# A 16-head causal attention with a gated feed-forward layer: another fixed order on all five engines, and P*V of two units moved behind the next pair's first scores

## What is computed

```python
# attention, x: (4, 1024, 128), 16 heads of 64
q = (x @ Wq).reshape(B, N, H, Dh).transpose(0, 2, 1, 3)
kv = x @ Wkv                      # k and v alike
s = jnp.einsum('bhid,bhjd->bhij', q * scale, k)
gm = jnp.max(s, axis=-1, keepdims=True)          # over the whole row
p = jnp.where(causal_mask, 0.0, jnp.exp(s - gm))
out = jnp.einsum('bhij,bhjd->bhid', p, v) / (jnp.sum(p, axis=-1, keepdims=True) + EPS)
x = layernorm(x + out.reshape(B, N, H * Dh) @ Wo + bo)
# feed-forward: x_prev is x one token earlier
xr = mu_r * x + (1 - mu_r) * x_prev;  xk = mu_k * x + (1 - mu_k) * x_prev
r = sigmoid(xr @ W_r);  k_act = square(relu(xk @ W_k))
x = layernorm(x + r * (k_act @ W_v))
```

## Time and profile before

| | |
|---|---|
| median of 3 runs | 1035.9 us (1035.74 to 1036.77) |
| the profiled execution | 1036.35 us, its span 1034.6 us |
| busy share of the span | PE 93%, weight loads 67%, DVE 88%, ACT 68%, POOL 57% |
| granted TensorE clock | 0.993 of full speed on the mean |
| a usual step of the main loop | 29.7 us |
| main loop ends | at about 970 us; the rest is the tail |

### The profile page before, as it was taken

One profiled execution on the slowest core, in us unless ns is written; L12 is line 12 of the kernel. 1 busy time (PEld: TensorE's weight loads), 2 busy tenths in 40 slices (PEclk: granted clock), 3 DMA queues, 4 the chain that ended last, 5 costly groups with the idle time before them and its releaser, 6 DMA issues. The chain is left out here.

```text
span 1034.6 us, 24773 instructions
## 1 busy us (share of the span) xinstructions
PE 966.7 (93%) x8947; PEld 689.2 (67%) x8947; DVE 910.2 (88%) x1546; ACT 704.5 (68%) x1456; POOL 586.1 (57%) x918
## 2 busy tenths in 40 slices
PE   7799999999999999999999999999999999999895
PEld 5566666676766666667666666767666766666463
DVE  5989888998898899889889988898899889889957
ACT  4667667666676666667667666766666667667667
POOL 5345655565656556555655565665556556653363
PEclk9999999999999999999999999999999999999898
DMA  6255665556556545555564555556555555665432
GB/s 171 57 140 130 137 153 129 121 121 145 133 130 148 132 118 129 137 138 133 140 153 115 117 135 138 134 134 153 135 122 121 135 140 134 140 150 131 100 81 82
DMA packets 74218, 134.24 MB, mean 130 GB/s; under 512 B 26864, under 2 KB 36848, under 8 KB 74096
## 3 DMA queue, kind: packets, MB, share of 16 engines
q1 hardware_dynamic: 73520, 132.26, 54.6%
q10 hardware_dynamic: 576, 0.39, 0.2%
HBM read 21.17 MB, written 2.36 MB: 23 GB/s over the span
## 5 line engine op out<-in xcount | busy, mean ns | idle before, releaser
L879 DVE TENSOR_SCALAR_CACHE_REDUCE tile<-ps 128x1024 f32<-128x1024 f32 x512 | 599.5, 1217 | 90.7 <-PE ps L1137 90.5
L682 ACT ACTIVATE tile<-tile,neg_max 128x640 f32<-128x640 f32 (+7 forms) x512 | 393.3, 770 | 128.7 <-POOL tile L487 128.6
L1137 PE MATMUL ps<-ks,qs 64*128 64x512 f32 x3072 | 398.8, 397 | 9.3 <-DVE tile L879 3.8
L1137 PEld LDWEIGHTS ps<-ks,qs 64*128 64x128 f32 x3072 | 294.4, 184 | 73.1 <-issue 28.9
L487 POOL TENSOR_SCALAR_AFFINE_SELECT tile<-tile 128x128 f32<-128x128 f32 x512 | 151.1, 295 | 302.9 <-DVE tile L879 302.8
L1250 PE MATMUL ps<-pt,vs 128*64 128x256 f32 (+1 forms) x2560 | 264.6, 361 | 0.8 <-DVE tile L879 0.5
L888 DVE STREAM_TRANSPOSE stage<-tile 128x640 f32<-128x640 f32 (+3 forms) x256 | 250.5, 1015 | 0.0
L1250 PEld LDWEIGHTS ps<-pt,vs 128*64 128x64 f32 x2560 | 173.7, 137 | 101.8 <-DVE tile L879 14.2
L1176 PE MATMUL ps<-xs,ws 64*128 64x512 f32 x744 | 119.5, 425 | 22.4 <-DVE tile L879 16.9
L495 POOL TENSOR_TENSOR ot<-ot,rb 128x512 f32<-128x512 f32 x64 | 101.6, 1588 | 55.5 <-issue 54.5
L689 ACT ACTIVATE x1t<-ps 128x1024 f32<-128x1024 f32 x31 | 31.9, 1028 | 125.4 <-PE ps L1176 125.4
(11 more groups left out here) (91 smaller groups left out, 587.5 us busy)
## 6 DMA issues: line engine op xcount, KB each, us to landing
pt<-stage SPq DMA_DIRECT2D x512, 120.0 KB, 3.2
pt<-stage SPq DMA_DIRECT2D x512, 88.0 KB, 2.1
rb<-recips SPq DMA_DIRECT2D x64, 256.0 KB, 4.1
y<-in_L_attn_x SPq DMA_DIRECT2D x3, 512.0 KB, 8.7
out<-y SPq DMA_DIRECT2D x3, 512.0 KB, 3.2
pt<-in_L_attn_Wkv SPq DMA_DIRECT2D x2, 384.0 KB, 6.8
pt<-in_L_attn_x SPq DMA_DIRECT2D x2, 256.0 KB, 4.4
wos<-in_L_attn_Wo SPq DMA_DIRECT2D x1, 512.0 KB, 7.2
```

What stands on the lines that cost most here:

```text
L682: act.activation(cols, cols, ACT.Exp, bias=neg_max[:, at:at + 1], scale=-1.0, accum_out=sums[:, p % 2, a, t:t + 1]).then_inc(s_exp, 1)
L879: dve.tensor_scalar(tile[:, at, :], place_for(("scores", p, t, a))[:, :], -SCALE, None, ALU.mult, ALU.min, accum_out=neg_max[:, at:at + 1] ...
L1137: ins = mm(place_for(("scores", p, t, a))[:, c * HALF:(c + 1) * HALF], qs[rows, p % 2, qh, t * P:(t + 1) * P], ks[rows, p % 2, kh, c * HAL ...
```

## The change

It has three parts. The set of instructions of the loop stays the same; all of them are moved.

**PE's list and the places.** K's projection of the next pair comes first in step k and alternates half by half with v's; q's two halves stand around scores 2; the output projection's two halves stand around group 2, late in the step. PV0 of pair k moves to step k+1, behind its scores 0. PV1 of the pair before moves up, behind scores 4, and scores 5 is cut in its halves by group 1. The table `FOLLOWS` is new throughout; the parts of it that matter here: k follows PV0, q follows scores (1, 0), scores (3, 0) follows q, group 1 follows PV1, scores (7, 0) follows the output projection, scores (7, 1) group 2.

**The other lists.** DVE, ACT and POOL get the order that goes with it. DVE's transposes of tiles 6 and 7 of a pair now stand behind the next step's first readings. `norm(k-1, 1)` stands between the masks of tile 7 on POOL.

**SP's list.** The moves of units 2 and 3 stand together, and the two DMAs of the reciprocals come behind the last move of unit 3.

**The tail.** PV0 of pair 31 comes behind the loop and takes the first place in `LATE`; on ACT `take_out(30)` and `take_values(31, 0)` stand ahead of the first square root.

```diff
 FOLLOWS = {
-    ("scores", 3, 0,): (("out",), 2),
+    ("scores", 3, 0,): (("q",), -1),
-    ("scores", 7, 0,): (("pv", 0,), 0),
-    ("scores", 7, 1,): (("scores", 6, 1,), 0),
-    ("q",): (("scores", 0, 0,), 1),
-    ("k",): (("scores", 2, 1,), 1),
+    ("scores", 7, 0,): (("out",), 2),
+    ("scores", 7, 1,): (("group", 2,), 0),
+    ("q",): (("scores", 1, 0,), 1),
+    ("k",): (("pv", 0,), 2),
-    ("group", 1,): (("scores", 3, 1,), 0),
+    ("group", 1,): (("pv", 1,), 1),
...
-LATE = [("out", LAST, 0), ("pv", LAST, 1), ("pv", LAST, 2), ("out", LAST, 1), ("sum", 3, 0), ("sum", 3, 1)]
+LATE = [("pv", LAST, 0), ("out", LAST, 0), ("pv", LAST, 1), ("pv", LAST, 2), ("out", LAST, 1), ("sum", 3, 0), ("sum", 3, 1)]
...
+                move(k, 2, 0)
+                move(k, 2, 1)
+                move(k, 2, 2)
+                move(k, 2, 3)
+                move(k, 3, 0)
+                move(k, 3, 1)
+                move(k, 3, 2)
+            move(LAST, 3, 3)
             column_recips(LAST)
-            move(LAST, 3, 0)
             spread_recips(LAST)
-            move(LAST, 3, 1)
-            move(LAST, 3, 2)
-            move(LAST, 3, 3)
...
             mask(LAST, 7, 1)
             add_out(LAST - 2, 1)
+            norm(LAST - 1, 0)
             norm(LAST - 1, 1)
...
+            take_out(LAST - 1)
+            take_values(LAST, 0)
             deviations(0, 0)
             take_last_sums(0)
...
-            turn_sums()
             project_out(LAST - 1, 0)
             project_out(LAST - 1, 1)
+            values(LAST, 0, (0, 1))
+            turn_sums()
             turn_normed(0, 0)
```

More of the change, by code:

```diff
@@ L44 @@
 LAST = ALL_PAIRS - 1
+SUMS_IN = "kq"
 def x_half(p):
@@ L514, in _ @@
             for k in range(ALL_PAIRS):
+                if k >= 1:
+                    mask(k - 1, 0, 0)
+                if k >= 1:
+                    mask(k - 1, 0, 1)
+                if k >= 1:
+                    mask(k - 1, 1, 0)
+                if k >= 1:
+                    mask(k - 1, 1, 1)
+                if k >= 3:
+                    norm(k - 3, 0)
+                if k >= 1:
+                    mask(k - 1, 2, 0)
+                if k > 0:
+                    split(k, 0)
+                if k >= 1:
+                    mask(k - 1, 2, 1)
+                if k >= 1:
+                    mask(k - 1, 3, 0)
+                if k >= 1:
+                    mask(k - 1, 3, 1)
+                if k > 0:
+                    split(k, 1)
+                if k >= 1:
+                    mask(k - 1, 4, 0)
+                if k > 0:
+                    split(k, 2)
+                if k >= 1:
+                    mask(k - 1, 4, 1)
+                if k >= 1:
+                    mask(k - 1, 5, 0)
+                if k >= 1:
+                    mask(k - 1, 5, 1)
                 if k > 0:
                     split(k, 3)
+                if k >= 3:
+                    add_out(k - 3, 0)
+                if k >= 1:
+                    mask(k - 1, 6, 0)
                 if k >= 1:
@@ L520, in _ @@
                     mask(k - 1, 7, 0)
+                if k >= 2:
+                    norm(k - 2, 1)
                 if k >= 1:
                     mask(k - 1, 7, 1)
[L523 to L540, removed]
                 if k >= 3:
                     add_out(k - 3, 1)
[L543 to L549, removed]
+            mask(LAST, 0, 0)
+            mask(LAST, 0, 1)
+            mask(LAST, 1, 0)
+            mask(LAST, 1, 1)
+            norm(LAST - 2, 0)
+            mask(LAST, 2, 0)
+            mask(LAST, 2, 1)
+            mask(LAST, 3, 0)
+            mask(LAST, 3, 1)
+            mask(LAST, 4, 0)
+            mask(LAST, 4, 1)
+            mask(LAST, 5, 0)
+            mask(LAST, 5, 1)
+            add_out(LAST - 2, 0)
+            mask(LAST, 6, 0)
             mask(LAST, 6, 1)
@@ new lines, in _ @@
+            evacuate(LAST, 2, 0)
+            evacuate(LAST, 2, 1)
+            evacuate(LAST, 3, 0)
+            evacuate(LAST, 3, 1)
+            evacuate(LAST, 4, 0)
+            recips_of(LAST - 1)
+            evacuate(LAST, 4, 1)
+            weights_of_mix()
+            evacuate(LAST, 5, 0)
+            evacuate(LAST, 5, 1)
+            turn_tile(LAST, 4, 0)
+            turn_tile(LAST, 4, 1)
+            evacuate(LAST, 6, 0)
+            evacuate(LAST, 6, 1)
+            first_moments(0)
@@ L1346, in _ @@
                 if k < LAST:
+                    project_qk(k + 1, "k", 0)
+                else:
+                    turn_half(0, 0)
+                project_values(k, 0)
+                if k < LAST:
+                    project_qk(k + 1, "k", 1)
+                else:
+                    turn_half(0, 1)
+                project_values(k, 1)
+                if k < LAST:
                     project_qk(k + 1, "q", 0)
                 else:
-                    turn_half(0, 0)
+                    turn_half(1, 0)
+                scores(k, 2, 0)
+                scores(k, 2, 1)
                 if k < LAST:
```

272 lines of the change are left out of this document (137 added, 135 removed).

## The result

The changed kernel takes **1051.95 us** (median of 4 runs, 1051.63 to 1054.22) against 1035.82 us for the kernel before in the same session (4 runs, 1035.32 to 1036.77). The ratio is 1.0159, 95% interval 1.0146 to 1.0172: slower by 1.6%. The forecast was 1045.5 us, in a range of 1034 to 1056. The profiled execution took 1052.2 us with a span of 1050.3 us, 15.7 more than the 1034.6 before, and all that follows accounts for these 15.7.

A forecast was written before the change was run, and what follows sets the result against it. PE, hardly ever stopping, was taken to bound the loop. The loop's -10.4 us and the tail's +20.2 us gave +9.8 us on the profiled 1036.35 us, 1045.5 us after allowing 0.45 us for the median; range 1034 to 1056 us.

The forecast's parts named there:

- the clock's rival: Tail: half clock after PE's two stops slows PV0 by 2.3 us and later work by some 3; 1051 us, chance 0.15.
- Gone, -1.4 us a step: Main loop: alternating k and v, and moving other calls between halves, removes PE waits of 1.4 us a step.
- New, behind q, 0.7 us: Each step, ahead of scores 3: PE waits 0.7 us for ACT's copy of q, covered only by group 0.
- The first rival: Main loop: steps are shorter than forecast, 28.5 us if q's copy is ready; 1024 to 1034 us, chance 0.15.
- New, ahead of scores 6, 0.25 us: Each step: scores 6 wait 0.25 us for the place of scores (5, 1), which DVE must read first.
- A usual step, 29.25 us: Main loop: 28.3 us of PE work plus waits of 0.7 and 0.25 us, 0.46 us less than before.
- Six steps with turned tokens, 1.55 us each: Group 1 waits for ACT's copies and DVE's subtraction: 0.6 us work and 0.95 us wait extra in each.
- Step 0 is bound by DVE in both, 0: First step of the loop: DVE bounds it before and after the change, so its time changes by 0 us.
- The tail (a) to (c), 22.8 us: Later pair 30 output projection, table load 13.9 us later, reciprocals behind 16 moves: norm (31, 0) starts 22.8 us later.
- the second rival: Tail: reciprocals are no bound if PE and POOL find work during SP's moves; 1036.6 us, no change, chance 0.13.
- (d), 2.6 us given back: Tail, after norm (31, 0): work gathered during the wait is then ready and gives back 2.6 us.
- The steps gain nothing: Main loop: PV2 waits for SP's moves, or scores 6 and 7 for readings; 29.75 us steps, 1060 us, chance 0.15.

The follow-up runs named there:

- kernel 6: Changed kernel with the second half of q's projection ahead of scores 2, next to the first: 1074.23 us.
- kernel 7: Changed kernel with k's two halves side by side and v's two behind them, alternation undone: 1070.59 us.
- kernel 8: Changed kernel with 20 and 28 matmuls of no use in step 0, where PV1 and PV2 stand in later steps: 1049.78 us.
- kernel 5: Changed kernel with DVE subtracting turned tokens ahead of its reading of scores (4, 1), not behind it: 1044.03 us.
- kernel 11: Kernel 10 with 16 more matmuls of no use in each of steps 0 and 1, where the output projection stands in later steps: 1025.17 us.
- kernel 1: Changed kernel with the last pair's reciprocals sent behind unit 2's moves and fetched behind unit 3's first 4 moves, as before: 1042.50 us.
- kernel 2: Changed kernel with ACT's first two square roots ahead of the copies of pair 30's output and PV0 of pair 31: 1040.01 us.
- kernel 3: Changed kernel with the edits of kernel 1 and kernel 2 together: 1036.91 us, ratio 1.0002 to before.
- kernel 4: Kernel before with only the last pair's reciprocals going out and back behind all 16 moves of unit 3: 1045.33 us.
- kernel 9: Changed kernel with the edits of kernel 1, kernel 2 and kernel 5: 1027.52 us, ratio 0.9923 to before.
- kernel 10: Kernel 9 with the matmuls of no use of kernel 8 in step 0: 1026.56 us, ratio 0.9904 to before.

## Why the prediction came out as it did

The sign and the mechanism held: the loop gained, the tail lost more, by the chain that was foretold, and the time lay in the range. It lay above the 1040 to 1050 us that the forecast alone reaches. That the clock's rival says 1051 us is luck: it counted stops of the tail, and much of what was missed lies in the first steps. 1051.95 - 1045.5 = 6.5 us were missed, by these steps:

- **Gone, -1.4 us a step: right in kind, too small.** I priced a pair side by side against half of a pair of scores, 1.53 us. The measure of a projection without the wait is its own, 1.38 us, so both pairs together cost 0.9 us and not 0.6. Kernels 6 and 7 give 0.33 to 0.34 for one pair moved back: a pair takes 1.71 to 1.72 us there and took 1.83 in the kernel before, and no run shows where that last 0.1 us comes from.
- **New, behind q, 0.7 us: right** (0.75, in every step and in kernels 7 and 8). That the place of scores (2, 0) sets a floor only 0.3 us below it I didn't see; kernel 6 showed it. The first rival (steps under 28.9 us) falls with it, by a little: 29.03.
- **New, ahead of scores 6, 0.25 us: the wrong place.** The wait is 0.4 us, one call earlier, ahead of the output projection. It inherits from scores (4, 1), and scores 6 then come late enough for theirs.
- **A usual step, 29.25 us: 29.03.** This gave 30 x 0.22 = 6.6 us that I hadn't counted on, and it hid as much of the misses below: that the loop's sum came near is in part luck, errors that cancel.
- **Six steps with turned tokens, 1.55 us each: mis-sized, 2.35.** The wait is 1.64 us, where I had 0.95, and scores 6 and 7 wait for readings on top: +0.8 each, 4.8 us over the six. Kernel 5 took back 7.2.
- **Step 0 is bound by DVE in both, 0: this failed.** PE has less to do in it than before, since PV0 of pair 0 left it, and stands in front of scores 5; its clock falls. +1.85 us, and a low clock in step 1 costs 2.8 more (34.2 us, against 31.4 for a token step); step 10 lost 1.0, at a granted clock of 0.89 on the mean of the 15 us from 330. The step that failed is the one that put PE's clock at nothing in the loop: I looked for it only in the tail. Kernels 8 and 11, with the stops of step 0 filled, run it at the full clock and begin step 1 at 41.13 and 41.31 us.
- **The tail (a) to (c), 22.8 us: right in each link, 20.9.** The output projection at 37.35 (38.5 predicted), the table load at 45.8 (46.9), the end of the last transpose at 52.9 (54.4), 16.8 us from there (17.1). My 17.1 was a little below its own terms: 8.2 + 8 us and at least 1 for the landing make 17.2 to 18.7. Kernels 1 to 4 show both causes, one by one and together: the second rival falls with kernels 1 and 4, in which SP's order alone took back 9.5 us and cost 9.2.
- **(d), 2.6 us given back: failed.** The work was ready, and the last output projection started 1.57 us after norm instead of 2.78. But it took 2.08 us instead of 1.02, and PV1 3.80 instead of 2.60, at a clock of 0.51: +2.3 us. The clock's rival was right on this stop. Behind the first one PV0 took 2.38 us, and that was luck: the same two stops (8.4 and 1.1 to 1.2 us) stand in the profiles of all eleven kernels with the new order, and PV0 took 2.38 us in four of them (after, 6, 7, 9) and 3.77 to 4.53 in seven.
- **The steps gain nothing: wrong.** PV2 never waited for SP's moves in a usual step.

In sum, step 0 +1.85, the loop +2.8 (-6.6 + 4.8 + 3.8, and 0.8 because the 24 usual steps take 29.06 us on the mean and not 29.03), the tail +1.2: 5.9 us in the span. The rest is how the two profiled executions lie to their medians, and a slip: 1036.35 + 9.8 - 0.45 is 1045.7, not 1045.5. What I hadn't joined up is that a long stop which the new order opens in the loop can be paid for twice, once as a wait and once as slow matmuls behind it.

## What to carry to other kernels

When a loop is reordered, write its last pass separately and keep there the order that its consumers need: here two DMAs behind twelve moves in one pass of 32 cost 9 us, more than the 7.5 that the loop's new order won. Price a wait by the instruction's own time without it, not by that of a similar one. And count what follows a stop on PE at the half clock as well as at the full one, in the first steps too, where a reordering takes the work away that kept PE running. A single profile can fall on either side: compare the same stretch in several kernels before giving its difference to an edit.

## What the hardware showed that I had not expected

**A loop that looks busy can drop to the half clock.** After: PE stops for 2.35 us in step 0, the granted clock is 1.00 up to 32.0 us and 0.50 from 32.5 to 38.5, and the 24 matmuls in that stretch take 4.64 us instead of 3.0. The stops of 0.66 and 0.76 us lie inside the low stretch and came too late to cause it. In kernel 8 the clock fell near 64 us, behind a stop of 1.56 us in step 1 and ahead of one of 1.41, and the same 24 matmuls took 5.25 us.

**The same stops don't always do it.** In the kernel before, two stops of 1.88 and 1.94 us stand close together ahead of step 1, and the clock stays at 1.00. PV0 of pair 31 is the case above: 2.38 us after and 4.53 in kernel 5, behind equal stops and with the same program in the tail; the clock was back at 1.00 when it began in the one and came back only at its end in the other. Kernels 9 and 10 have equal stops in step 1 (0.4, 0.2 and 1.6 us). In 9 the 24 matmuls behind them take 3.06 us, in 10 they take 4.61:

```profile
67.18 3.06 PE L1203 MATMUL ps<-ks,qs 64*128 64x512 f32 x24 [1.60 <-DVE tile L906]
```

```profile
65.29 4.61 PE L1203 MATMUL ps<-ks,qs 64*128 64x512 f32 x24 [1.60 <-DVE tile L906]
```

Kernel 9 had been low in step 0 and kernel 10 hadn't. The Trainium skill (TensorE: Matmul & The Clock Gate, What's actually happening) says that the clock falls after idleness and comes back after sustained work. Both rows lie behind the same idleness, so that sentence alone doesn't tell them apart, and no run here settles what does.
